# GpSimd scatters without fills between them, slot loads, row copies and pad fills in another order, the second tile table in fewer steps

## The reference

```
x = layernorm(x + attention(x, W_Q, W_K, W_V))          # causal softmax, d = 128
logits = (x @ gate_w + gate_b) / 0.9
keep the 2 largest of 8, softmax over them              # gate_probs
h = gelu(x @ w1[e] + b1[e])                             # 128 -> 512, exact gelu
expert_out = h @ w2[e] + b2[e]                          # 512 -> 128
out = sum over the 2 experts of gate_prob * expert_out
out = layernorm(out) * ln_g + ln_b
x = layernorm(x + out)
```

## Time and profile before

| | |
|---|---|
| median of 3 runs | 287.6 us (287.13 to 287.66) |
| the profiled execution | 285.26 us, its span 283.5 us |
| TensorE busy | 235.7 us, 83% of the span |
| GpSimd busy | 178.6 us, 63% |
| ScalarE, VectorE busy | 181.3 us (64%), 171.8 us (61%) |
| the fills of `pause` (L1280) | 131, 255 ns each |
| scatters to `slots` (L1287) | 64, 970 ns each |
| scatters to `returned` (L1294) | 71, 1057 ns each |
| a returned result, issue to landing | 2.7 us, 71 of them |
| a loaded pair of 256 KB, issue to landing | 3.8 us, 16 of them |
| share of the chain that ended last | GpSimd 32%, TensorE 30% |

### The profile page before, as it was taken

How to read it: one execution, slowest core, us unless ns; L and a number is a source line. 1 busy time by engine, 2 the same in 40 slices (tenths; PEclk the granted TensorE clock), 3 DMA queues, 4 the chain that set the end, 5 groups by cost and what they waited for, 6 DMA issues and landing times.

```text
span 283.5 us, 7517 instructions
## 1 busy us (share of the span) xinstructions
PE 235.7 (83%) x1867; PEld 213.9 (75%) x1868; DVE 171.8 (61%) x947; ACT 181.3 (64%) x537; POOL 178.6 (63%) x296
## 2 busy tenths in 40 slices
PE   2898998999997697999999999999967999992000
PEld 2566876878876486999989999999957999992000
DVE  0047577788888764459532333565247759976984
ACT  3265848777756378888874655555534589778733
POOL 8200028488888888888888888888887565657000
PEclk9999999999999759999999999999999999998555
DMA  4999102212212525332338778674189797331722
GB/s 121 273 327 283 42 2 84 68 49 75 85 49 83 143 58 144 77 79 65 94 85 260 230 266 270 177 225 129 46 275 339 270 275 253 145 107 46 224 81 75
DMA packets 44802, 42.38 MB, mean 149 GB/s; under 512 B 5440, under 2 KB 33520, under 8 KB 44768
## 3 DMA queue, kind: packets, MB, share of 16 engines
q1 hardware_dynamic: 40448, 33.10, 39.9%
q0 software_dynamic: 4320, 8.92, 9.1%
HBM read 27.89 MB, written 12.01 MB: 141 GB/s over the span
## 4 chain that ended last, share of the span: by engine, by line
POOL 32%; PE 30%; issue 10%; ACT 9%; DVE 8%; DMA 5%; SPq 3%; DVEq 1%; ACTq 1%; POOLq 0%
POOL returned L1294 15%; POOL slots L1287 11%; PE bank L555 8%; PE bank L544 8%; POOL pause_out L1280 6%; PE bank L409 3%; ACT pair L695 3%; DMA slot_x<-slots 2%; PE bank L395 2%; PE bank L436 2%; PE bank L457 2%; ACT h L690 2%; PE bank L400 1%; PE bank L476 1%; DMA slots<-rows,slot_of 1%
## 5 line engine op out<-in xcount | busy, mean ns | idle before, releaser
L690 ACT ACTIVATE h<-bank,b_cols 128x128 f32<-128x128 f32 x284 | 81.2, 370 | 48.9 <-PE bank L544 48.1
L1294 POOL DMA_INDIRECT returned<-x,slot_back x71 | 75.0, 1057 | 30.2 <-POOL pause_out L1280 18.6
L555 PE MATMUL bank<-w_all,h 128*128 x568 | 78.7, 282 | 0.0
L544 PE MATMUL bank<-slot_xT,w_now 128*128 128x128 f32 x568 | 77.1, 280 | 0.9 <-issue 0.9
L1287 POOL DMA_INDIRECT slots<-rows,slot_of x64 | 62.1, 970 | 17.8 <-POOL pause_out L1280 17.5
L544 PEld LDWEIGHTS bank<-slot_xT,w_now 128*128 128x128 f32 x568 | 71.3, 197 | 1.1 <-issue 1.1
L555 PEld LDWEIGHTS bank<-w_all,h 128*128 128x128 f32 x568 | 69.0, 192 | 1.0
L1280 POOL MEMSET pause_out<- 1x200 f32 x131 | 33.4, 255 | 34.2 <-DVE rows L912 34.0
L818 DVE CAST slot_back<-slot_x 128x1 uint32<-128x1 f32 x71 | 10.7, 151 | 53.2 <-PE bank L544 52.9
L777 DVE TENSOR_REDUCE negmax<-bank 128x1 f32<-128x128 f32 (+3 forms) x32 | 14.7, 485 | 19.4 <-PE bank L410 19.1
L476 PE MATMUL bank<-ident,slot_x 128*128 128x128 f32 x71 | 20.6, 291 | 6.0 <-DMA slot_x<-slots 6.0
(11 more groups left out here) (160 smaller groups left out, 313.1 us busy)
## 6 DMA issues: line engine op xcount, KB each, us to landing
w_now<-in_L_ffn_w_dram SPq DMA_DIRECT2D x47, 256.0 KB, 4.0
slot_x<-slots SPq DMA_DIRECT2D x71, 65.0 KB, 2.8
w_all<-in_L_ffn_w_dram SPq DMA_DIRECT2D x16, 256.0 KB, 5.6
pair<-returned SPq DMA_DIRECT2D x16, 256.0 KB, 3.8
x<-n_L_attn_embeddings_dram SPq DMA_DIRECT2D x8, 256.0 KB, 4.1
rows<-rows SPq DMA_DIRECT2D x8, 256.0 KB, 2.7
returned<-x,slot_back POOLq DMA_INDIRECT x71, 2.7
slots<-rows,slot_of POOLq DMA_INDIRECT x64
```

The costliest lines, as they stand in the source:

```text
L544: m = nc.tensor.matmul(o, w1_now[:, s, cols], slot_xT[:, s % RING, :], start=True, stop=True)
L555: m = nc.tensor.matmul(o, h[:, s % RING, c * P:(c + 1) * P], w2_c, start=False, stop=(c == FC - 1))
L690: m = nc.scalar.activation(h[:, s % RING, cols], bank_[:, cols], ACT.Gelu, bias=b1_cols[:, c:][:, bass.ds(first, 1)])
L1294: g_.indirect_dma_start(returned, bass.IndirectOffsetOnAxis(ap=slot_back[:, j:j + 1], axis=0), y[:, j % Y_RING, :], None).then_inc(y_retur ...
```

## The change

GpSimd's `pause` goes, all 131 of them, with its tile and its semaphore. Nothing else on GpSimd changes.

On SyncE four things change their place. Of the first eight tile loads, the one of tile 4 now waits until ScalarE has copied the first part of the last sequence's transposed probabilities (`pT_ready`), the one of tile 5 until it has copied all of them, and the row copy of sequence 6 stands ahead of tile 6 instead of tile 4. The row copy of sequence 7 stands behind the load of tile 10 instead of tile 7. The 8 pad fills no longer stand in a row behind tile 23 and a wait for the second table; each stands behind one of the loads of tiles 16 to 23 (`PADS_IN` = 2, the third group of eight), and their rows are read from `pad_at` ahead of tile 16, behind a wait for a new semaphore, `pads_known`, that VectorE raises with the first instruction of `rest_table`.

On VectorE the 12 pieces of `rest_table` are spread over steps 8 to 13 instead of 8 to 15: four in the first step, and two in the last.

```
             for s, at in enumerate(first_rows):
                 if s == AHEAD + 1:
+                    sp.wait_ge(pT_ready, (B - 1) * UNITS + 1)
+                elif s == AHEAD + 2:
+                    sp.wait_ge(pT_ready, B * UNITS)
+                elif s == AHEAD + 3:
                     copy_rows(B - 2)
                 load_slots(s, at)
-            copy_rows(B - 1)
...
             def pad_rows():
+                sp.wait_ge(pads_known, 1)
...
+                pads = pad_rows() if i == PADS_IN else []
...
                     load_slots(s, at[s])
+                    if i == PADS_IN:
+                        fill_pads(s, pads[s])
+                    if j == UNROLL + AHEAD - 1:
+                        copy_rows(B - 1)
...
             sp.wait_ge(numbers_ready, 2)
-            for e, at in enumerate(pad_rows()):
-                fill_pads(e, at)
...
-                    vec.tensor_copy(pad_at[:], running[0:1, B % 2, :])
+                    vec.tensor_copy(pad_at[:], running[0:1, B % 2, :]).then_inc(pads_known, 1)
...
-                        for q in ((0, 1), (2, 3), (4, 5), (6, 7), (8,), (9,), (10,), (11,))[s]:
+                        for q in ((0, 1, 2, 3), (4, 5), (6, 7), (8,), (9,), (10, 11), (), ())[s]:
...
-            def pause(n):
-
-                g_.memset(pause_out[:], 0.0).then_inc(paused, 1)
-                pool.wait_ge(paused, n)
-
             def dispatch(b, t):
                 for k in range(TOPK):
-                    pause((b * TB + t) * TOPK + k + 1 + (RETURNS_AHEAD if b == B - 1 else 0))
...
             def give_back(j):
-                if j < J - 4:
-                    pause(NT * TOPK + j + 1 if j >= RETURNS_AHEAD else NT * TOPK - TB * TOPK + j + 1)
                 pool.wait_ge(y_ready, j + 1)
```

More of the change, by code:

```diff
@@ L22 @@
 W1_AHEAD = 2
-PAUSE = 200
 TEMPERATURE = 0.9
@@ L56, in moe_block @@
     BOUND = FULL // UNROLL
+    PADS_IN = BOUND - 1
     BLOCKS = 2 * E - 1
@@ L79, in moe_block @@
         unused = sb("unused", [P, 1])
-        pause_out = sb("pause_out", [1, PAUSE])
         expert_id = sb("expert_id", [P, E])
@@ L206, in moe_block @@
         dispatch_ready, numbers_ready = sem("dispatch_ready"), sem("numbers_ready")
+        pads_known = sem("pads_known")
         dispatched = [sem(f"dispatched{g}") for g in range(2)]
@@ L1239, in _ @@
             made = sem("made")
-            paused = sem("paused")
             g_ = nc.gpsimd
```

## The result

The changed kernel takes 276.1 us, the median of 4 runs (275.33 to 279.57), and the kernel before, now with 4 runs, 287.37. The ratio is 0.9619, with a 95% interval of 0.9542 to 0.9695. The forecast was 278.0, between 275.5 and 283.5. The execution profiled after took 276.57 us, its span 274.8.

The account below looks back on a forecast made before the run. GpSimd, always behind at 1.50 us a scatter, was taken to cause TensorE's waits at the start, tile 25 and tile 53. Savings of 2.3 + 1.8 + 5.5 = 9.6 us took 287.6 to 278.0 us, range 275.5 to 283.5.

Parts of the forecast that it names:

- The scatter without its fill: GpSimd's scatter period falls from 1.50 to 1.26 us, saving 0.24 us each; bounds 0.96 and 1.54 us.
- Start: First tile loads: sequence 3's last scatter lands sooner, TensorE reaches sequence 6's rows earlier; 2.3 us saved, bounds 0 to 3.0.
- The clock's part: At the start, transposes and gate matmuls run less at the lower TensorE clock: up to 1.2 us, half taken.
- Tile 25: TensorE's wait there goes because the last dispatch ends at 132.8 and lands at 134.4 us: 1.8 us saved.
- The new wait: SyncE's `pads_known` wait ahead of tile 16's load: costs nothing, with 3.0 us to spare.
- cover: SyncE and VectorE edits carry no term but belong to the sum, since pads would otherwise be late next.
- Tile 53: Earlier returns shorten SyncE's hold from 12.3 to some 3 to 4 us: 5.5 us saved, bounds 0 to 5.7.
- The 16 us of lead: At tile 53, SyncE's tile loads run eight steps (16 us) ahead, so its remaining hold does not stop TensorE.
- Tail: After the last gelu, ScalarE and VectorE decide and nothing waits for GpSimd: cost 0, between -0.5 and +0.5 us.
- The unpaused period near 1.5: Rival: GpSimd's scatter period stays near 1.5 us, all three waits end as before: 287.4 us, chance 0.06.
- the crowd at tile 53: Rival: loads queue on the DMA engines, tiles or pairs are late, up to 5.5 us stay: 283.5 us, chance 0.10.
- The slow rival: GpSimd scatters without a gap hold each other up, period 1.77 us: 308 us, deciding above 1.50 us; chance 0.07.

Follow-up runs that it names:

- the second profile: Another profiled execution of the unchanged changed kernel, with TensorE at about half clock near 50 us: 279.84 us, in a group of runs with median 277.25 us.
- e5: Changed kernel with the fills put back before the 32 dispatches of sequences 0 to 3 alone: 279.32 us, ratio 0.9743.
- e7: Changed kernel with fills of 100 zeros, half the old size, before all scatters but the last four returns: 275.81 us, ratio 0.9660.
- e1: Kernel before with its 131 fills removed and nothing else changed, so with the old SyncE and VectorE orders: 276.51 us, ratio 0.9733.
- e2: Changed kernel with the fills put back before all scatters but the last four returns: 286.09 us, ratio 1.0004.
- e4: Changed kernel with fills before the returns (but the last four) and none before dispatches: 276.74 us, ratio 0.9702.
- e3: Changed kernel with fills before the 64 dispatches and none before returns: 280.39 us, ratio 0.9806.
- the candidates: Changed kernel with VectorE's and ScalarE's work on returned results two steps sooner, 275.34 us; or three steps sooner plus two pieces of VectorE's tail moved, 273.28 us.
- e6: Changed kernel with fills of 400 zeros, twice the old size, before all scatters but the last four returns: 300.08 us, ratio 1.0454.
- e8: Changed kernel with VectorE's eight two-input additions of ln_b replaced by a one-input sum: all eight returns there 0.96 us, one execution 279.8 us.

## Why the prediction was right

**The scatter without its fill.** 1.26 us was taken from two of three intervals, and it held for the dispatches too, which wait for nothing in between. The lower bound of 0.96 did not come: the 0.30 us is there without a wait.

**Start.** 2.3 us predicted, 2.53 measured. The mechanism of the larger part was the one given: TensorE's arrival at sequence 6's rows is then set by ScalarE. That part was put at 1.76 us and is 1.6 in every trace without the fills. The clock's part was a choice between bounds, 0.6 us taken of 1.2, and there the close fit is luck: it is 0.9 us of gain in the execution profiled after and 0.7 us of loss in the second profile, so that the start gives 2.5 us in the one and 0.9 in the other. The prediction did not foresee that this part depends on the execution. e5 shows the term alone at 2.74, and in e7 nothing of it is lost at a period of 1.41.

**Tile 25.** 1.8 predicted, 1.80 measured. The last dispatch was to end at 132.8, so to begin at 131.5, and began at 132.91, 132.1 less the 0.85 us of the head. The table's additions did hold two scatters, by 0.81 and 1.45 us, 2.3 together where the prediction had allowed up to 1.8.

**The new wait.** SyncE's queue in the changed kernel has tile 16's load at 121.78:

```profile
121.78 0.33 SPq L296 DMA_DIRECT2D slot_x<-slots  x1
```

The tile is transposed at 127.89. With 2.8 us for the load 3.3 us are left, where the prediction had 3.0. It cost nothing.

**What the prediction had wrong in this part** is the sentence that the SyncE and VectorE edits belong to the sum as cover. "The pads would then be next" is true, but by 0.18 us (e1). The same holds for the other moves on SyncE. Without the fills they are worth nothing that the times show, and with them neither (e2).

**Tile 53.** 5.5 predicted, 5.49 measured. GpSimd was even with the results at tile 24, predicted 26. SyncE was held 3.5 us, predicted 3 to 4, but this figure does not follow from the prediction's own working: a wait from 188.9 to the 190.3 at which it had tile 38 back is 1.4 us. The result of tile 38 came later than its 186.3, as its return shows,

```profile
189.19 1.15 POOL L1293 DMA_INDIRECT returned<-x,slot_back  x1 [0.85 <-DVE x L1052]
```

and the first pair was issued at 193.05. The 16 us of lead took up that error of about 2 us. What the prediction did not see is that the fills before returns had no part of their own in it: e4 keeps them and loses nothing, e3 has the other ones and loses nothing either. The gap needs both.

**Tail.** 0 predicted, 0.16 us more measured, which I cannot tell from chance. It hangs on ScalarE and VectorE, as the candidates show: only moving their own work shortened it.

**The sum.** 9.6 predicted, 9.55 by the trace from the mark on. The medians differ by 11.3 (287.37 and 276.1). The rest of about 1.7 us is no part of the mechanism that the traces show; the stretch up to tile 8 varies by more than that between executions, and the interval of the ratio, times 287.37, leaves a gain of 10.9 us anywhere from 8.8 to 13.2. In the group of the second profile the medians differ by 8.9 us only (286.18 and 277.25). The forecast of 278.0 lies 1.9 us above the first median and 0.75 above the second. What sets that part I have not settled.

**Rivals.** The unpaused period near 1.5 and the crowd at tile 53 did not come. The slow rival gave 308 us for a period of 1.77; e6 with 1.66 took 300. From 1.50 on it added 14 us for 0.16 us of period, and the rival's 20 for 0.27 were of the right kind, if on the low side. So its mechanism and its point were right, and its condition false: the return of 1.47 us was VectorE's doing, not crowding (e8). There the trace agrees with the Trainium skill, "SBUF — State Buffer", "Who interferes with whom": a VectorE instruction with two SBUF inputs contends with a GpSimd instruction that reads SBUF. The same section's inference that such an addition does not hold up a DMA's descriptors does not cover these indirect scatters: beside the addition of ln_b they took 0.2 us longer in the changed kernel, and 0.5 us in the one before.

## What to carry to other kernels

An engine that is late all the time may cost nothing or all of its lateness: find the two or three places where another engine really waits for it, and work out there how much lead it needs. Between 1.41 and 1.50 us a scatter lay 10 us, and from 1.26 to 1.41 nothing. Once such an engine is early, look at once for the work that was placed late on its account: moving the results' work three steps and two pieces of the tail gave another 3 us by the trace. And before a small term is read from one trace, look at a second execution of the same kernel: here one stretch of it differed by 1.6 us.

## What the runs showed of the hardware

A GpSimd indirect scatter of 128 rows keeps 0.30 us between two of its kind, whether or not a wait stands there, and takes 0.96 us besides; a fill and a wait on it added 0.15, 0.24 and 0.40 us for 100, 200 and 400 numbers. A VectorE addition with two on-core inputs that is under way when it starts makes it longer by what is left of the addition less 0.12 us, 1.15 to 2.41 us in the changed kernel, even where the addition works on one partition alone; a reduction as long with one input does not. And the same program has executions that reach the mark 1.65 us apart, with a stretch at about half of TensorE's clock near 50 us in the later one. Those with that stretch also take 1.6 us more from the mark to tile 8, with a granted clock of 0.64 instead of 0.89 from 102 to 114 us, while all that follows tile 8 agrees to 0.1 us.
